# Causal zeros in the exponentials: GpSimd selects in place of mask matmuls under the scores

## The reference

```
att = einsum('bhtd,bhsd->bhts', q, k) / sqrt(16)
att = where(tril, att, -inf)
att = softmax(att, axis=-1)
y   = einsum('bhts,bhsd->bhtd', att, v)
```

## Time and profile before

| what | us |
|---|---|
| median of 3 runs | 1697.62 |
| lowest and highest | 1686.34 to 1700.3 |
| the profiled execution | 1696.44 |
| its span | 1694.6 |
| PE, DVE, ACT, POOL busy | 1518.0, 940.5, 836.4, 432.1 |
| mean granted TensorE clock | 0.957 |

### The profile page before, as it was taken

How to read it: one execution, slowest core, us unless ns; L and a number is a source line. 1 busy time by engine, 2 the same in 40 slices (tenths; PEclk the granted TensorE clock), 3 DMA queues, 4 the chain that set the end, 5 groups by cost and what they waited for, 6 DMA issues and landing times. The chain is left out here.

```text
span 1694.6 us, 30471 instructions
## 1 busy us (share of the span) xinstructions
PE 1518.0 (90%) x12028; PEld 1155.9 (68%) x12064; DVE 940.5 (55%) x1939; ACT 836.4 (49%) x1395; POOL 432.1 (25%) x562
## 2 busy tenths in 40 slices
PE   2799999978889999999999999987999999976997
PEld 2577776755666878788888877855655555545997
DVE  4456667745545252423425344366667788755886
ACT  0145556655544545455454464534544443435674
POOL 0002355521120010102202022042221223242766
PEclk9699999999988999899999999998999999987999
DMA  3646777752422203020220202223674354004542
GB/s 90 90 83 124 150 133 130 129 100 48 69 45 39 33 7 51 1 39 8 38 39 1 39 2 44 39 39 56 123 152 118 73 106 94 28 26 149 174 142 72
DMA packets 98894, 123.99 MB, mean 73 GB/s; under 512 B 8285, under 2 KB 88900, under 8 KB 96193
## 3 DMA queue, kind: packets, MB, share of 16 engines
q1 hardware_dynamic: 96240, 117.44, 35.1%
q0 software_dynamic: 1792, 3.94, 0.7%
q10 hardware_dynamic: 720, 0.66, 0.1%
HBM read 48.86 MB, written 9.51 MB: 34 GB/s over the span
## 5 line engine op out<-in xcount | busy, mean ns | idle before, releaser
L1007 DVE TENSOR_REDUCE mx<-mslot 128x4 f32<-128x1024 f32 x192 | 234.6, 1222 | 215.1 <-PE mslot L565 214.2
L833 ACT ACTIVATE probs<-eslot 128x1024 f32<-128x1024 f32 x192 | 196.6, 1024 | 164.5 <-PE eslot L590 134.8
L1211 POOL TENSOR_SCALAR ave<-amv 128x2 f32<-128x2 f32 x64 | 15.7, 246 | 965.6 <-DVE amv L930 611.0
L1005 DVE TENSOR_REDUCE mx<-mslot 128x2 f32<-128x256 f32 (+1 forms) x256 | 130.5, 552 | 224.1 <-PE mslot L565 223.0
L590 PE MATMUL eslot<-stack 50*128 50x256 f32 (+2 forms) x1280 | 158.1, 326 | 10.2 <-ACT probs L833 9.3
L590 PEld LDWEIGHTS eslot<-stack 50*128 50x128 f32 (+1 forms) x1280 | 98.8, 191 | 98.5 <-issue 67.6
L565 PE MATMUL mslot<-stack 48*128 48x256 f32 (+2 forms) x1280 | 141.8, 301 | 10.7 <-DMA stack<-split 9.7
L831 ACT ACTIVATE probs<-eslot 128x512 f32<-128x512 f32 (+1 forms) x256 | 111.6, 488 | 76.1 <-PE eslot L590 75.1
L605 PE MATMUL bank<-probs,v 128*32 128x256 f32 (+1 forms) x2048 | 131.4, 370 | 0.0
L653 PE MATMUL bank<-hidden,l 128*128 128x256 f32 x512 | 114.0, 381 | 0.0
L565 PEld LDWEIGHTS mslot<-stack 48*128 48x128 f32 (+1 forms) x1280 | 102.1, 195 | 14.8 <-issue 10.7
(11 more groups left out here) (219 smaller groups left out, 3180.2 us busy)
## 6 DMA issues: line engine op xcount, KB each, us to landing
stack<-split SPq DMA_DIRECT2D x240, 256.0 KB
w<-in_w SPq DMA_DIRECT2D x16, 1024.0 KB, 5.3
slot_rows<-hTf SPq DMA_DIRECT2D x4, 650.0 KB, 8.8
slot_rows_sb<-slot_rows SPq DMA_DIRECT2D x4, 650.0 KB, 7.1
expert_rows<-slot_rows SPq DMA_DIRECT2D x8, 260.0 KB, 2.7
xb<-in_x SPq DMA_DIRECT2D x8, 256.0 KB, 9.0
l<-in_l SPq DMA_DIRECT2D x2, 1024.0 KB, 9.8
qk<-in_ctx SPq DMA_DIRECT2D x8, 256.0 KB, 6.0
```

The lines of the kernel that those rows point to most:

```text
L833: e = act.activation(PR[:, k, :, :, :].rearrange("p a k q -> p (a k q)"), ps[:, :, :, :].rearrange("p a k q -> p (a k q)"), ACT.Exp, scale ...
L1005: a = dve.tensor_reduce(MX[:, qt, :, p], ps[:, :, qt, 0:(qt + 1) * P], AX.X, ALU.max)
L1007: a = dve.tensor_reduce(MX[:, :, :, p].rearrange("p q a -> p a q"), ps[:, :, :, :], AX.X, ALU.max)
```

## The change

The masks under the scores for the exponentials are left out in layers 0 and 2 (layer 4's stay). The exponentials of the diagonal blocks are taken unmasked, and a new step "trim" on POOL sets those above the diagonal to zero in `probs` by one `affine_select` of 128 x 512 f32 for each pair. It stands behind "exp" in its slot. The exponentials of key tile kt are now written from column 0 on, so that both diagonal blocks lie at columns 0 to 127. The mix waits for the trim of its second pair and moves one slot later (13 + p) in layers 0 and 2. Since a unit's last mix now stands behind the step "v read" of the unit three later, both writers of the values wait for that mix. `causal_k`, its DMA and its cast are gone. The masks for the maxima stay.

```
-                put(at(11 + p), MASK, "exp mask", u, p)
+                if l in CAUSAL:
+                    put(at(11 + p), TRIM, "trim", u, p)
+                else:
+                    put(at(11 + p), MASK, "exp mask", u, p)
...
-                put(at(12 + p), MIX, "mix", u, p)
+                put(at((13 if l in CAUSAL else 12) + p), MIX, "mix", u, p)
...
         def mask_for_exp(u, p):
...
             for a in range(2):
-                if l == 4:
-                    pe.matmul(ps[:, a, :, :], ident_b[:, :], NK[u % RING][:, :, :], start=True, stop=False)
-                else:
-                    for kt in range(TT):
-                        pe.matmul(ps[:, a, kt, kt * P:(kt + 1) * P], ident_b[:, :], causal_k[:, :],
-                                  start=kt == 0, stop=False, skip_group_check=True)
+                pe.matmul(ps[:, a, :, :], ident_b[:, :], NK[u % RING][:, :, :], start=True, stop=False)
...
         def scores_for_exp(u, p):
...
-            if l not in MASKED:
+            if l != 4:
                 slot_for_exp(u, p)
...
         def mix_four(u, g):
...
-            pe.wait_ge(*exped.at(u, 2 * g + 1))
+            pe.wait_ge(*(pool_step.at("trim", u, 2 * g + 1) if l in CAUSAL else exped.at(u, 2 * g + 1)))
...
-                                   PR[:, (2 * g + j // 2) % 4, j % 2, kt, q0:S], start=kt == 0, stop=kt == TT - 1)
+                                   PR[:, (2 * g + j // 2) % 4, j % 2, kt, 0:S - q0], start=kt == 0, stop=kt == TT - 1)
...
-                    e = act.activation(PR[:, k, :, kt, kt * P:S], ps[:, :, kt, kt * P:S], ACT.Exp, scale=0.25)
+                    e = act.activation(PR[:, k, :, kt, 0:S - kt * P], ps[:, :, kt, kt * P:S], ACT.Exp, scale=0.25)
...
                 act.wait_ge(*bank_filled.at("v", u))
+                if layer(u - RING) in CAUSAL:
+                    act.wait_ge(*bank_filled.at("o", u - RING, PAIRS // 2 - 1))
...
             dve.wait_ge(*bank_filled.at("v", u))
+            if u >= RING and layer(u - RING) in CAUSAL:
+                dve.wait_ge(*bank_filled.at("o", u - RING, PAIRS // 2 - 1))
...
+            elif step == "trim":
+                pool.wait_ge(*exped.at(u, n))
+                diagonal = PR[:, n % 4, :, :, 0:P].rearrange("p a k q -> p (a k) q")
+                pool.affine_select(diagonal, diagonal, [[0, 2 * TT], [1, P]], ALU.is_ge, 0.0, base=0, channel_multiplier=-1)\
+                    .then_inc(*pool_step("trim", u, n))
```

More of the change, by code:

```diff
@@ L103, in build @@
             routed_mixture(nc, ctx, t, known, slots_dram, shared)
-ENDS, MASK, EXP, MAX, WEIGHT, OTHER, MIX = range(7)
+ENDS, MASK, EXP, TRIM, MAX, WEIGHT, OTHER, MIX = range(8)
 MIXTURE_UNITS = range(2 * B, 3 * B + 3)
@@ L204, in attention_layers @@
     causal_q = sb("causal_q", [P, P], BF16)
-    causal_k = sb("causal_k", [P, P], BF16)
     rope_swap = sb("rope_swap", [P, P])
@@ L343, in _ @@
             sp.dma_start(Y[:, 0, 0:P], t["causal_q"]).then_inc(consts_in, 16)
-            sp.dma_start(Y[:, 1, 0:P], t["causal_k"]).then_inc(consts_in, 16)
             sp.dma_start(Y[:, 0, P:2 * P], t["upto"]).then_inc(consts_in, 16)
@@ L347, in _ @@
                 sp.dma_start(dst.ap(), t[name]).then_inc(consts_in, 16)
-            sp.wait_ge(consts_in, 16 * (len(CONSTS) + 3))
+            sp.wait_ge(consts_in, 16 * (len(CONSTS) + 2))
         @block.gpsimd
@@ L368, in _ @@
             dve.memset(CLEAR[:, TOKEN:WIDE], 1.0)
-            dve.wait_ge(consts_in, 16 * (len(CONSTS) + 3))
+            dve.wait_ge(consts_in, 16 * (len(CONSTS) + 2))
             for b in range(B):
@@ L375, in _ @@
             dve.tensor_copy(causal_q[:, :], Y[:, 0, 0:P])
-            dve.tensor_copy(causal_k[:, :], Y[:, 1, 0:P])
     block = ctx.enter_context(nc.Block())
@@ L540, in mask_for_exp @@
         def mask_for_exp(u, p):
-            l = layer(u)
             slot_for_exp(u, p)
@@ L590, in scores_for_exp @@
                     mm = pe.matmul(ps[:, a, kt, q0:S], keys(u, h, k)[:, kt * P:(kt + 1) * P],
-                                   queries(u, h, k)[:, q0:S], start=l in (1, 3), stop=l in (1, 3) or kt == TT - 1,
-                                   skip_group_check=l in CAUSAL)
+                                   queries(u, h, k)[:, q0:S], start=l != 4, stop=l != 4 or kt == TT - 1)
             mm.then_inc(*exp_filled(u, p))
@@ L1788, in layouts @@
     out["causal_q"] = np.where(i[None, :] > i[:, None], f(LOW), f(0)).astype(f)
-    out["causal_k"] = np.ascontiguousarray(out["causal_q"].T)
     out["upto"] = (i[:, None] <= i[None, :]).astype(f)
```

## The result

The changed kernel takes 1716.8 us, a median of 4 runs (1712.2 to 1724.8); the kernel before took 1695.1 us beside it (4 runs). The ratio is 1.0133, 95% interval 1.0095 to 1.0172: slower by 1.3%, where the prediction said 0.4% faster (1691). The profiled executions have spans of 1694.6 and 1723.1 us, 28.5 us apart (the medians are 21.7 apart), so the profiles can show where the time went. One execution of all those used here, of the sixth experiment's kernel, ran at a mean clock of 0.73 and took 1976.8 us; the ratio of that kernel leaves it out.

A forecast was written before the change was run, and what follows sets the result against it. TensorE was taken as the bound, except where VectorE's 2.18 us loop closes layer 0's slots. Layer 0 +4, layer 2 -10.7, GpSimd's queue +0.6: -6.1 us, median 1691 us, range 1676 to 1720.

The forecast's parts named there:

- rival (d): TensorE's granted clock falls more often behind layer 0's emptier slots: three or four slow slots, +10 us, 1701; chance 0.07.
- slot 0: Layer 0's slot with shift and k, of eight per unit: mask out, mix in, 3.57 to 4.15 us.
- empty slot: Layer 0 slot without a larger TensorE job (1, 2, 7): VectorE's loop keeps it at 2.18 us, masks worth nothing.
- the tail: Layer 0's last eleven pairs, taken with its first few: some slots gain, others pay for the mix, -0.4 us together.
- The wait of the v write: Values written only after the last mix three units back: just fits, nothing, at most some 0.2 us.
- Slot 4: Layer 0's slot with the v projection: mask out, mix in, 3.03 to 3.61 us.
- slot 6: Layer 0's slot with the q projection: mask out, mix in, 3.04 to 3.62 us.
- -8.9 summed: Layer 2's 46 pairs beside experts: masks out -9.7 us, waits for a bank VectorE reads +0.8.
- queue effects on h and T: Layer 2: a select ahead of the centring in GpSimd's queue delays h and T, +0.3 in two units, +0.6 us.
- (a): GpSimd becomes the bound in layer 0 if a select takes 2.6 us: +35, 1726 us; chance 0.17.
- (b): Every mask is worth 0.21 us or more and the mix's move is free: 27 us gained, 1671; chance 0.09.
- (c): Layer 2: a select and VectorE's small routing operations contend on SBUF, delaying experts: +7, 1698 us; chance 0.09.

The follow-up runs named there:

- sixth experiment: Changed kernel with the mix back in slot 12+p in layer 0 alone, the late mix and its waits kept in layer 2: 1702.2 us, ratio 1.0025.
- first experiment: Changed kernel with the mix back in slot 12+p and the waits before the value writes removed: 1698.9 us, ratio 1.0007 to the kernel before.
- third: Changed kernel with 10 to 16 unused small bf16 matmuls added at the end of layer 0's slots 3, 7 and 1: 1706.2 us, ratio 1.0059.
- seventh: Changed kernel with the mix back in slot 12+p and filler matmuls in layer 0's slots 1, 7 and 2: 1691.6 us, ratio 0.9968.
- second: Kernel before, masks kept and no selects, with the mix one slot later and the waits before the value writes: 1719.4 us, ratio 1.0111.
- fifth: Changed kernel without its 128 selects, late mix kept, entries above the diagonal left unmasked: 1715.1 us, ratio 1.0092 to the kernel before.
- fourth: Changed kernel with selects in layer 2 only, masks kept in layer 0, mix in slot 12+p in both: 1688.0 us, ratio 0.9947.
- tenth: Selects in all of layer 2, masks kept in layer 0, mix in slot 12+p, run once more: 1688.6 us, ratio 0.9928.

## Why the prediction was wrong

**The step that failed** is the sum's silent assumption, and the price and the chance given to rival (d). Every slot was added up at 2.4 GHz, because the clock had been 1.00 from 95 to 233 us before; the fall was rival (d), "three or four" slots, 10 us, 0.07. It came in slot 0 of all four full units from 119 to 197 us (5.64 to 5.70 us, 1.6 over the 4.02 at full clock), and five times more from 216 to 291 us, in layer 0's end: the slot from 215.59 us took 7.40 us at a clock of 0.54. A slot wholly at the lower level costs what the rival said (5.29 - 2.80 = 2.5 us in the first experiment, 2.7 in the prediction); it was their number, and the chance of any, that were set too low. The filler experiments give its price: 1.0133 - 1.0059 = 0.74% or 12.5 us (third), 1.0007 - 0.9968 = 0.39% or 6.6 us (first against seventh, intervals overlapping), both net of what the filler itself takes. Between the first two landmarks it is 19.2 - 6.2 = 13 us in the profiles. The prediction had the fact for it in hand: it wrote that a mask in an empty slot is worth nothing, which is to say that TensorE idles there instead, and it took mixes out of those slots too. The idle time in an empty slot was 0.75 us before and is now up to 1.13, in more slots.

The Trainium skill (TensorE: Matmul & The Clock Gate, "A second HAM failure mode: psum-queue depth-cycling") describes a kernel in which short idle gaps between groups of matmuls, repeated often enough, make the clock go back and forth. This case's traces agree in kind: the gaps here are 0.34 to 1.13 us, and the falls come behind them.

**The second term that was mis-sized** is the tail, "-0.4 together". It is +14.0, and three parts of it can be named; they overlap, and no run separates them fully.

- The wait of the v write, priced at "nothing" for layer 0's own loop. In layer 1 the writer is ScalarE, which has y's input to read behind it, and the late mix holds the write for 1.8 to 2.3 us. TensorE's wait of y for ScalarE's `o` was 0.5 us in all before, and is 0.5 in each of the seven kernels with layer 0's mix at its old place; it is 4.3 in the changed kernel, and 3.7, 4.2 and 4.2 in the second, third and fifth, which have the move. That is 3.8 us, three of the four waits in the tail. The move and its wait were never run apart.
- The selects in GpSimd's queue. The prediction saw the new wait there and priced it for h and T alone; it fell on VectorE's shift. Without selects the tail is +7.7 us in the fifth kernel and +7.2 in the second, with 3.1 us less of waits for `max_parts` in the fifth.
- The clock: the third kernel, with selects and filler, has 9.7 instead of 14.0. Without selects it falls less too, 0.92 instead of 0.81 from 255 to 300 us, so the 6.3 us between the changed and the fifth kernel are not the selects' waits alone.

The second and fifth kernels' 7.2 and 7.7 us less their waits of y (3.2 and 3.8) leave some 4 us that stay open.

**What was right, point by point.** Empty slots of layer 0: 2.18 us, as predicted. Slot 4: 3.69 (3.61 predicted); slot 6: 3.69 (3.62); slot 5: 2.18 (2.18); slot 0 at full clock: 4.02 (4.15); the unit at full clock 22.3 (22.28). The move alone, masks kept, slows the unit to 22.96. Layer 2: 6.48 us for the slot of 6.71 (6.50 predicted), and -10.9 us from the first gate to layer 4's first mask (-8.9 summed), in the changed kernel's profile. Single profiles of the other kernels with selects in layer 2 give that stretch -1.3 to -11.2 us, and the second kernel, which kept every mask, -2.6, so the closeness is in part luck and the timed ratios of the fourth and tenth kernels are the stronger evidence. Select: 0.637 us at the median, by the low bound (0.617) and not the 1.2 taken; queue effects on h and T: 8.7 us of waits for h against 6.9 before, and 9.2 against 10.7 for y, so +0.3 where +0.6 was taken.

**The rivals.** (a), GpSimd as the bound, is out: it is busy 23.3 of 43 us from 190 to 233 us, and a select takes half of the 1.3 us from which (a) decides. (b), the whole 27 us, is out: in layer 0 with the mix at its place and the clock held, the unit gains 0.7 to 1.2 us of 8 x 0.21. (c) did not come where it was placed: layer 2 gains. But its mechanism, the two engines holding each other up, is in the traces of layer 0's end (fifth experiment), and its sign came true: `max_parts` grew from 0.17 to 1.1 us at its longest, and VectorE's busy time from 940.5 to 949.0 us (940.4 without selects). A part of the loss is this rival's. (d) was the right kind of cause. The time of the changed kernel is the forecast's slot sum, plus the clock, plus the tail with its two waits.

## What to carry to other kernels

Work on TensorE that lies under another engine's loop is free, but it may be what holds the granted clock: before taking it out, ask where the idle time goes, and what matmul slot stands behind it, since that slot can cost almost twice its time. A change that frees one engine is best made only in the stages where that engine is the bound: selects in layer 2 alone, with layer 0 as it was, beat both kernels, the old one by 0.5 to 0.7% and, by the two ratios, the new one by about 2%. An operation added to an engine's queue also moves what stands behind it: ask what that will now run beside, on the other engines. And a wait added for a buffer three units back is priced where the stage changes, by what stands behind it in the queue of each engine that writes the buffer, not in the steady loop.

## What was not expected of the hardware

Adding matmuls made a kernel faster whose TensorE is busy 88% of the span: beyond the intervals once, within them once. A granted clock of 0.50 takes eight 128x256 f32 matmuls from 2.0 to 3.8 us, behind idle gaps none of which was longer than 1.13 us in that layer's full units. Where the fall comes depends on the schedule (slot 0 of every unit in the changed kernel, the v slot of every second unit with the mix back), and it repeats there in step with the units. A select of 128x512 f32 in place on GpSimd takes 0.64 us, about as long as one-input arithmetic on as many elements, and one of them and an addition beside it stretched two VectorE operations of 128x32 from 0.17 and 0.19 to 1.09 and 0.56 us.
